# The first load of x issued from ScalarE instead of SyncE in a three-layer scoring kernel

## The reference

```python
h1 = leaky_relu(layer_norm(x1 @ W1.T))      # x1, x2 = x[:, :F], x[:, F:]
h2 = leaky_relu(layer_norm(x2 @ W1.T))
h1 = leaky_relu(layer_norm(h1 @ W2.T)); h2 = leaky_relu(layer_norm(h2 @ W2.T))
h = leaky_relu(layer_norm(concat([h1, h2]) @ W3.T))
y = h @ W4.T
```

## Time and profile before

| | us |
|---|---|
| median of 3 runs | 232.88 |
| lowest, highest | 232.81, 232.94 |
| the profiled execution, its own time | 233.68 |
| span of the profiled execution, first to last instruction | 231.9 |
| TensorE busy in the span | 224.6 (97%) |
| VectorE busy | 191.4 (83%) |
| ScalarE busy | 151.7 (65%) |

### The profile page before, as it was taken

One profiled execution on the slowest core, in us unless ns is written; L12 is line 12 of the kernel. 1 busy time (PEld: TensorE's weight loads), 2 busy tenths in 40 slices (PEclk: granted clock), 3 DMA queues, 4 the chain that ended last, 5 costly groups with the idle time before them and its releaser, 6 DMA issues.

```text
span 231.9 us, 2894 instructions
## 1 busy us (share of the span) xinstructions
PE 224.6 (97%) x999; PEld 179.3 (77%) x999; DVE 191.4 (83%) x245; ACT 151.7 (65%) x240; POOL 28.8 (12%) x41
## 2 busy tenths in 40 slices
PE   6999999999999999999999999999999999999992
PEld 2678786888887888888868888888888878888772
DVE  2689999978959999997669699999989699979324
ACT  3797989859588598963678453665546484824630
POOL 0000020020100200000012224427001400000014
PEclk9999999999999999999999999999999999999995
DMA  5999999999879999446839958668677414150000
GB/s 178 370 378 373 409 341 294 347 272 343 290 214 371 340 276 296 171 161 230 300 54 231 291 164 275 228 212 245 215 251 251 148 69 128 56 181 1 3 0 1
DMA packets 17950, 51.93 MB, mean 224 GB/s; under 512 B 2772, under 2 KB 3156, under 8 KB 17936
## 3 DMA queue, kind: packets, MB, share of 16 engines
q1 hardware_dynamic: 16064, 48.86, 60.5%
q0 software_dynamic: 1872, 2.89, 8.0%
HBM read 50.95 MB, written 0.01 MB: 220 GB/s over the span
## 4 chain that ended last, share of the span: by engine, by line
PE 82%; DMA 5%; DVE 4%; ACT 4%; issue 1%; POOL 1%; SPq 1%; POOLq 0%; DVEq 0%
PE acc L1004 79%; DMA xe_raw<-x 5%; PE acc L1126 2%; DVE xe_lo L703 2%; ACT xe_hi L588 2%; ACT unused L542 1%; DVE x_sum L758 1%; PE acc L1139 1%; ACT xt_hi L588 1%; DVE x_sum L768 1%; ACT we_hi L548 0%; POOL inv L485 0%; ACT stage L548 0%; PE acc L1147 0%; PE acc L1155 0%
## 5 line engine op out<-in xcount | busy, mean ns | idle before, releaser
L1004 PE MATMUL acc<-xe_lo,we_hi 128*128 128x512 f32 x176 | 68.8, 391 | 0.3 <-DVE xe_lo L703 0.2
L1004 PE MATMUL acc<-xe_hi,we_lo 128*128 128x512 f32 x176 | 68.5, 389 | 0.0
L703 DVE TENSOR_TENSOR xe_lo<-xe_raw,xe_hi 128x1024 fp32r<-128x1024 f32 (+1 forms) x48 | 55.6, 1177 | 15.2 <-ACT xe_hi L588 15.1
L588 ACT CAST xe_hi<-xe_raw 128x1024 fp32r<-128x1024 f32 (+1 forms) x48 | 47.9, 1009 | 30.7 <-PE acc L1004 22.1
L1004 PE MATMUL acc<-xe_hi,we_hi 128*128 128x512 f32 x176 | 48.3, 391 | 0.0
L1004 PEld LDWEIGHTS acc<-xe_lo,we_hi 128*128 128x128 f32 x176 | 33.0, 188 | 8.4 <-issue 1.7
L1004 PEld LDWEIGHTS acc<-xe_hi,we_hi 128*128 128x128 f32 x176 | 32.9, 188 | 7.4 <-issue 0.7
L1004 PEld LDWEIGHTS acc<-xe_hi,we_lo 128*128 128x128 f32 x176 | 33.1, 188 | 6.7
L588 ACT CAST xt_hi<-x_sum 128x2048 fp32r<-128x2048 f32 x14 | 26.7, 1910 | 12.8 <-DVE x_sum L774 12.8
L703 DVE TENSOR_TENSOR xt_lo<-x_sum,xt_hi 128x2048 fp32r<-128x2048 f32 x14 | 32.0, 2289 | 1.9 <-ACT xt_hi L588 1.9
L1004 PE MATMUL acc<-xt_lo,ws_hi 128*128 128x512 f32 x64 | 25.0, 391 | 0.1
(11 more groups left out here) (107 smaller groups left out, 274.4 us busy)
## 6 DMA issues: line engine op xcount, KB each, us to landing
xe_raw<-x SPq DMA_DIRECT2D x51, 512.0 KB, 5.5
xs_raw<-x SPq DMA_DIRECT2D x14, 768.0 KB, 5.8
stage<-w SPq DMA_DIRECT2D x21, 256.0 KB, 5.8
x_sum<-x SPq DMA_DIRECT2D x10, 256.0 KB, 3.4
x_sum<-x SPq DMA_DIRECT2D x4, 512.0 KB, 4.5
x_sum<-x POOLq DMA_DIRECT2D x4, 512.0 KB, 8.0
xe_raw<-x SPq DMA_DIRECT2D x2, 256.0 KB, 4.2
stage<-w SPq DMA_DIRECT2D x2, 128.0 KB, 3.3
```

The lines of the kernel that those rows point to most:

```text
L588: act.copy(hi_of(u, part), raw_of(u, part)).then_inc(hi_ready[part.buffer], 1)
L703: dve.tensor_tensor(lo_of(u, part), raw_of(u, part), hi_of(u, part).bitcast(F32), ALU.subtract)\
L1004: return pe.matmul(acc[:, bank, :], w, x, start=first, stop=True, skip_group_check=True)
```

## The change

ScalarE waits for `zeros_ready` and issues the load of X0a on its own DMA queue; SyncE issues one load less. Nothing else differs.

```diff
@@ block.sync
             sp.dma_start(w_raw[:, 0, 0:N1], w1[pair, :, 0:N1]).then_inc(first_w_landed, 16)
-            sp.dma_start(xe_raw[:, 0, 0:NC], first_half[:, 0:NC]).then_inc(first_x_landed, 16)
             sp.dma_start(xe_raw[:, 0, NC:], first_half[:, NC:]).then_inc(xe_landed[0], 16)
             sp.dma_start(w_raw[:, 0, N1:], w1[pair, :, N1:]).then_inc(w_landed[0], 16)
             load_half(1)
@@ block.scalar
             u = UNITS[0]
+
+            act.wait_ge(zeros_ready, 1)
+            act.dma_start(xe_raw[:, 0, 0:NC], x_half_of(0, u.pair, 0)[:, 0:NC]).then_inc(first_x_landed, 16)
             hi(u, u.parts[0])
             hi(u, u.parts[1])
```

## The result

The changed kernel takes 231.67 us (median of 22 runs, 231.20 to 233.47), the kernel before in the same job 233.12 us (22 runs, 232.32 to 234.40). The ratio is 0.9946 with a 95% interval of 0.9931 to 0.9961: a gain of 0.54%, 1.26 us (the medians differ by 1.45).

A forecast was written before the change was run, and what follows sets the result against it. Bound by a start-up chain of loads and casts through X1 and half 5, then by TensorE from 39 us. Terms 0 + 0 + 0 - 0.23 us (stream) took 232.88 to 232.65 us, range 232.15 to 233.3.

The forecast's parts named there:

- Part (1), the slot: SyncE loses one issue of 0.47 us; X1's issue moves from 2.59 to 2.12, half 5's only with its wait.
- Part (2), ScalarE's issue and the table load: On ScalarE, the added wait and issue and the 1.28 us table load lie in idle time before 5.26: cost 0.
- That the change might not do what it says: On ScalarE, the table load stays ahead of the issue, X0a comes a microsecond and more behind W0a; costs nothing.
- Part (3), X0a's landing: X0a lands 0.2 us or more earlier, or 0.8 later; earlier gains 0, later is covered on ScalarE and TensorE.
- Part (4), W0a: W0a shares the DMA engines with X0a, 0 to 0.7 us later, within VectorE's 1.42 us idle time: cost 0.
- Part (5), the stream: Earlier issues fill idle DMA time from 2.0 to 5.0; stream gains 0 to 0.47 us, 0.23 taken.
- The sign that I had named: DMA share from 3.5 to 5.0 should rise from a mean of 0.70 to about 0.85, otherwise (5) is wrong.
- The whole-slot rival: X1 and half 5 land 0.47 to 0.59 us earlier, giving 232.3 us; chance 0.27.
- The rival that nothing moves: The start-up chain waits for bytes, not issues, so X1 and half 5 land as before: 232.9 us; chance 0.24.
- Part (6), what it gives at the end: Half 5 lands 0.23 us earlier, its ScalarE cast starts at 16.03 instead of 16.26, and everything to 39 us follows.
- The cap of 0.33 us beyond X1's gain: ScalarE's own run is 0.33 us ahead of half 5, limiting the gain if the stream gained more than X1.
- The late-X0a rival: X0a, behind SyncE's backlog, lands after 6.80 and costs time: 233.7 us; slower by over 0.2%, including a disturbed stream, chance 0.15.

The follow-up runs named there:

- the filler kernel: Changed kernel plus a 1 KB filler load on SyncE where X0a's load stood, X0a staying on ScalarE's queue: 233.66 us, ratio 1.0025 against the kernel before.
- the held kernel: Changed kernel with TensorE's first real matmul held back to 6.33 until W0b's hi is there: 232.59 us, ratio 0.9969 against the kernel before.
- to 5.37 in the median: Changed kernel with TensorE's first real matmul held back to 5.37 until X0b's hi is there: 231.73 us, ratio 0.9938 against the kernel before.
- the second one after: The unedited changed kernel profiled again in a later job, in an execution of 231.52 us; median there 231.54 us, ratio 0.9944 against the kernel before.
- first profile: The unedited changed kernel as first profiled, in an execution of 232.81 us, over 1 us more than its median.
- on one queue: SyncE loads X0a and X0b as one 512 KB load and ScalarE issues nothing, edited from the changed kernel: 232.57 us, ratio 0.9969 against the kernel before.
- the control with 32 columns: Changed kernel, SyncE waiting before X0b for a VectorE memset of 32 columns that ends before its first issue: 231.40 us, ratio 0.9912 against the kernel before.
- 400 columns: Changed kernel, SyncE held back before X0b by a VectorE memset of 400 columns, X1 issued at 2.22: 232.49 us, ratio 0.9960 against the kernel before.
- 512 columns: Changed kernel, SyncE held back before X0b by a full-length pause, a VectorE memset of 512 columns, X1 issued at 2.34: 233.49 us, ratio 1.0013 against the kernel before.

## Why the prediction was wrong in size, and what its mechanism lacked

**Part (1), the slot.** Right: X1's issue moved from 2.59 to 2.11 and half 5's only with its wait, from 10.72 to 10.01.

**Part (2), ScalarE's issue and the table load.** Right, the table load stands behind the issue and both are covered. That the change might not do what it says fell away with it.

**Part (3), X0a's landing.** Right that an earlier one gives nothing: the filler kernel has X0a's cast at 3.83 and no gain. That the first matmul is free within a range is borne out, to 6.33 in the profile of the held kernel and to 5.37 in the median, there on a path that had become 2 us shorter; the median of the kernel held to 6.33 lost 0.6 to 1.05 us. What I missed is the clock: a TensorE idle for 4.9 us costs half speed afterwards.

**Part (4), W0a.** Right: 0.46 us later, inside the 0 to 0.7 us, and the first matmul not held up. By the rule of the Trainium skill ("DMA: Bandwidth & Descriptors", section "Queues, rings and completion order") W0a would be about 0.35 us later, by estimate. The traces don't settle it: with the same two first issues, at 0.74 and 0.96, W0a landed at 3.41 in both profiles of the change, but at 2.88 and 3.00 in the kernels with the first matmul held back and at 2.89 with the filler, against 2.95 before.

**Part (5), the stream: the step that failed.** I bounded what could be won by the share of time in which the DMA engines were not busy, 0.59 us from 2.0 to 5.0, and took 0.23. Measured are 1.26 us in the median and 2.23 us in half 5's cast from the profile before to the second one after (16.26 to 14.03). The sign that I had named came, the share from 3.5 to 5.0 rose from 0.70 to 1.17 and 1.05 and the rate from 206 to 321 and 355 GB/s: the earlier issues do fill that hole. But the hole didn't measure the gain, for two reasons. The first is that the share was the wrong column. An engine counts as busy while a packet takes long: before, 5.00 to 8.00 had a share of 0.95 and moved 314 GB/s, where the changed kernel's full stream has 1.03 and moves 412; the first profile even has a share of 1.58 from 4.5 to 5.0, with 309 GB/s. In bytes, the rows of 2 to 5 us lose (386 - 252) / 386 x 3 = 1.04 us against the 386 GB/s that stood beside them, 1.17 against 412, twice my upper end, and the 3 us behind them (412 - 314) / 412 x 3 = 0.71 us more.

The second is that the bytes are no bound either: together they make 1.9 us, which holds the 1.26 us of the median, but not the 2.23 us between the profiles. I took half 5 to land earlier only if the whole stream did. In fact a load lands with the last of its 16 parts, and these were up to 2.5 us apart: the term that the sum had at nothing is the spread among the DMA engines, which from the profile before to the second one after shrank by 1.86 us for X1 and by 1.41 us for half 5, while their first parts came only 0.22 and 0.82 us earlier.

The whole-slot rival failed for the same reasons: it took 0.47 us of issue time to be worth at most 0.47 to 0.59 us of stream. It was worth 0.7 us on one queue and 1.3 with the second, and holding the issues back by 0.23 us cost 2.1 by the medians. The rule of the Trainium skill ("DMA: Bandwidth & Descriptors", section "Issuing engines are not separate DMA queues") that another engine's issue only saves the sequencer's time, agrees with the filler kernel (the second queue alone gives nothing), but as a price it is too low here: 0.47 us of issue time saved went with 1.26 us, and by the rule the sum would have been 0.47 at the most. The rival that nothing moves is refuted.

**Part (6), what it gives at the end.** Right and the firmest part: what half 5's cast gains, the kernel gains, one for one, in 15 profiles. The cap of 0.33 us beyond X1's gain was never reached, as X1 and half 5 moved together (2.08 and 2.23 us in the second profile).

**The late-X0a rival.** Its mechanism is real, its price too low: with a landing at 9.12 I would have had a cost of 9.12 - 6.80 = 2.3 us, and the kernel lost 3.5 us against the one before. TensorE at half clock up to about 15 us is the likely rest; it wasn't separated.

**What stays open.** Why a delay of 0.1 us in the first issues costs 1 us. It isn't one load, nor the number of loads on the queue, and by the landings it is not the amount of bytes but how far a few of the 16 parts fall behind in the first microseconds, as I read it on engines that then stay behind. What makes a packet take 1 to 2 us there isn't shown by any run. The first and second profile of one and the same kernel differ by 1.4 us in X1's landing with SyncE's first six issues at the same times within 0.01 us, so it differs from one execution to the next. The counts say that early issues make the good case more frequent: below 232.0 us are 14 of 22 and 9 of 12 executions of the change and all 6 of the control with 32 columns, but 1 of 12 with 400 columns, none of 12 with 512 or with the filler, and 3 of 135 of the kernel before. Whether they also make the bad case milder, and what the second queue adds to the slot, wasn't separated.

## What to carry to other kernels

Read the stream's start in GB/s against the full stream's GB/s, not in busy share: the missing bytes show that there is something to win, and it can be a multiple of the issue slot. They don't bound it, as a load lands with its slowest part: compare what had been moved when the load landed with what had to be. Take more than one profile of a kernel whose executions differ by as much as the gain. In a kernel whose start is bound by its first loads, put the fewest and earliest issues on the queue that carries the stream, and let another engine issue one of them, early and a little behind the first. Then find the one event at which the start-up chain hands over to the dense part, and judge each variant by the time of that event.

## What the runs showed of the hardware that I had not expected

- A shift of SyncE's first issues by 0.11 and 0.23 us moved the time by 1.1 and 2.1 us, and with it the DMA rate from 2 to 5 us: 328 GB/s in the control, 294 with 400 columns, 256 with the full pause.
- A load lands with the last of its 16 parts, and at the start of a stream these can lie far apart: X1's within 0.64 us in one execution of the change and 1.78 us in another, with SyncE's issues at the same times. Single packets took 1.8 to 2.0 us where the median one took 0.08, and the spread was still there seven loads later.
- Two first loads issued at 0.73 and 0.74 on two queues took 1.4 us more (and 1.1 against another kernel of the same job) than issued at 0.74 and 0.96.
- A 256 KB load issued on ScalarE's own queue at 2.94, behind nothing on that queue but beside SyncE's backlog, took 6.19 us; issued at 0.96 it landed in 3.1 to 3.2. It landed behind the load that SyncE had issued at 2.57 (at 8.39) and ahead of the one of 3.04 (at 9.57): a queue of its own did not take it past the backlog.
- The granted clock was 0.50 for TensorE's first real matmuls after 4.9 us of idling, and 1.00 after 1.11 us and after 1.68 us, in the kernel held to 6.33.
